# Two graph layers over 128 graphs, float32 in hi and lo halves: an earlier KT_lo, paired h2 copies, a fifth PSUM bank in the ring, and the bias added elsewhere on GpSimd

## The chip, the cores and the metric

One core of a Trainium2 chip. The metric is device time in microseconds, median of the runs shown. Engines: TensorE (PE; its weight loads are PEld), VectorE (DVE), ScalarE (ACT), GpSimd (POOL), SyncE (SP, which issues nearly all DMAs here).

## What is computed

Input x is 128 graphs of 128 nodes with 512 features; adj is a 128x128 0/1 matrix. Two residual layers, each ahead of it a layer norm and a relu:

```python
h = relu(layernorm(x))
z_l, z_g, v = h @ W_lang.T, h @ W_grav.T, h @ W_V.T
A_l = max(zn @ zn.T, 0) * not_eye            # zn: rows of z_l by their norms
A_g = exp(-|z_g[n] - z_g[m]|^2 / (2 sigma^2)) * not_eye
K   = w_l * rows(A_l * adj) + (1 - w_l) * rows(A_g * adj)   # rows: divided by their sum
x   = x + (K @ v) @ W_O.T
h2  = relu(layernorm(x))
x   = x + (adj * adj).T @ h2 + bias
```

## The kernel before, in words

The graphs are taken in groups of four (GB = 4), so there are 32 groups and 32 iterations of one software pipeline; each engine has its own program (the functions `iteration` of SP, POOL, ACT, DVE and PE), and semaphores tie them. Every float32 product is made of three matmuls of fp32r halves (`passes`): hi*hi, hi*lo, lo*hi. A hi half is an ACT copy out of PSUM, a lo half a subtraction on DVE (or GpSimd for h2).

Iteration i on PE, in order:

- **y phase**: eight products y (`y_block`, L947; 3, 3, 6, 6, 9, 9, 12, 12 matmuls of 512 columns) of group i's transposed h with the two triangular halves of the similarity weights. ACT copies each to y_hi (L441), DVE subtracts to y_lo (L590). It waits for all four hT_lo of its group.
- **P phase**: 48 matmuls of 256 columns into p_ps (L994), with the four transposes of K of group i-1 in the middle (L957), which ACT copies to KT_hi (L531) and DVE turns into KT_lo (`kt_lo`, L657).
- **K_v**: K times v for group i-1 (`k_v`, 12 matmuls; waits for KT_lo), which DVE adds to x (`add`, L661).
- **v phase**: four products of 12 matmuls each, h times the folded V and O weights; v_hi on ACT (L478), v_lo on DVE (L590).
- **layer 1** of group i-2 (`layer1`, 12 matmuls), which DVE adds to x (`output`, L694) once GpSimd has added the bias (`add_bias`, L326).

The y, K_v, v and layer 1 products share a ring of four PSUM banks. The uses of the ring are numbered through, 20 in an iteration (8, 4, 4, 4), and `free(use)` (L931) lets PE write a bank once the use BANKS before it has been drained by DVE:

```python
def free(use):
    wait_for(pe, drained, use - BANKS + 1)
```

DVE's order in an iteration: y_lo 0 to 2, `sum_s` of group i-1 (L787), `mask_l`, y_lo 3, `mask_g`, `row_factors` (L635: a reduction and four operations on 128x8), y_lo 4 and 5, `combine` (K), `turn_blocks` 0 and 1 of group i+1, y_lo 6 and 7, `turn_blocks` 2 and 3, `x_stats` of group i+2 (L601, four), `kt_lo` of group i-1, the four `add` with their `stats`, the squared norms of group i (`diagonal`, `squares`), then for each b v_lo, `turned_lo` (hT_lo of group i+1, L610) and for b of 0 and 1 `turn_p`; last the four `output` of group i-2.

GpSimd's order: (L354) wait for both masks of group i-1, four `add_bias` of group i-2 (L326), four `h2_lo` of group i-2 (L341), the norm factors of two layer norms, `row_norms` (L347, L349), `mask_norms` (L332, behind a DMA). It reads x rows, bias and h2f in SBUF, never PSUM.

ACT's order in the v phase: for each b v_hi, then hT_hi of group i+1 (`turned_hi`, L432; the first waits for the DMAs that turn h), behind b = 1 `shift` (L514), and `h2_full` (L502, the second norm and relu) of group i-1:

```python
for k in {0: [], 1: [0], 2: [1, 2], 3: [3]}[b]:
    h2_full(i - 1, k)
```

`add_bias(g, b)` waits for `h2_full(g, b)`, which reads x before the bias is in. SP issues 16 DMAs that turn h blocks (L246) behind `turn_blocks`, the DMAs for P and the norms, the load of x two groups ahead and the stores.

## Time and profile before

| | us |
|---|---|
| median of 3 runs (1272.72 to 1273.73) | 1273.24 |
| the profiled execution, its own time | 1273.49 |
| its span, first to last instruction | 1271.8 |
| PE busy | 1216.1 (96%) |
| DVE busy | 1114.0 (88%) |
| ACT busy | 699.1 (55%) |
| POOL busy | 598.0 (47%) |

The mean granted clock of TensorE is 0.992 of full speed. A matmul's busy time overlaps that of the next, so 96% is the share of the span in which some matmul was in flight; how fast the stream goes is read from the distance between starts. Iterations 2 to 29 look alike. The rows further down are of the one that starts at 603.09 us and ends where the next begins, at 640.76 us.

### The profile page before, as it was taken

Reading aid. Unit: us, or ns where it says so; the run is one execution under the profiler, and the core shown is the slowest. Engines: PE = TensorE matmul, PEld = TensorE weight load, DVE = VectorE, ACT = ScalarE, POOL = GpSimd, SP = SyncE. Lnnn points to the kernel's source line nnn. Section 1 sums busy time; section 2 is a strip of 40 time slices with the busy share of each in tenths; the row PEclk is TensorE's granted clock in tenths of the full one; section 3 lists DMA queues with packets and bytes.
Section 4 is the critical chain, followed back from the end, with each engine's and each line's share of the span. In section 5 each row is a group of like instructions: output and inputs, shape, how many; then the busy total and the mean of one; then the engine's idle time right before and its main releaser. Section 6 shows DMA issues by size and latency. Waiting matters only on the chain.

```text
span 1271.8 us, 22830 instructions
## 1 busy us (share of the span) xinstructions
PE 1216.1 (96%) x6076; PEld 1021.3 (80%) x6076; DVE 1114.0 (88%) x1892; ACT 699.1 (55%) x1324; POOL 598.0 (47%) x991
## 2 busy tenths in 40 slices
PE   7998999999999999999999999999999999999995
PEld 7877888888888888788888888888888888878883
DVE  6577899889889989889989889988988998988878
ACT  6355555565555466555556555546645545655544
POOL 1213455454555554545545445545454554444445
PEclk9998999999999999999999999999999999999997
DMA  7122333434433343433343443343443334343202
GB/s 273 35 90 60 119 101 103 130 121 128 140 102 93 119 126 122 140 108 99 108 134 121 133 128 103 98 125 122 126 140 107 93 113 130 120 138 107 76 33 100
DMA packets 115457, 145.10 MB, mean 114 GB/s; under 512 B 20848, under 2 KB 52720, under 8 KB 115440
## 3 DMA queue, kind: packets, MB, share of 16 engines
q1 hardware_dynamic: 114864, 144.57, 36.7%
q10 hardware_dynamic: 576, 0.33, 0.1%
q8 instruction: 7, 0.11, 0.0%
q14 instruction: 10, 0.08, 0.0%
HBM read 62.46 MB, written 49.87 MB: 88 GB/s over the span
## 4 chain that ended last, share of the span: by engine, by line
PE 42%; DVE 33%; issue 12%; ACT 6%; DMA 2%; DVEq 1%; SPq 1%; POOL 1%; ACTq 0%; POOLq 0%
PE ring L944 40%; DVE h L606 6%; DVE bn L601 5%; DVE deg L637 3%; DVE deg L641 3%; ACT y_hi L441 2%; DVE deg L646 2%; DVE K L651 2%; ACT K L525 2%; DVE chain L787 2%; DVE chain L632 2%; SPq L246 1%; DVE KT_lo L657 1%; DVE x_ring L694 1%; DMA p_dram<-chain 1%
## 5 line engine op out<-in xcount | busy, mean ns | idle before, releaser
L944 PE MATMUL ring<-hT_hi,Lw_hi 128*128 128x512 f32 x640 | 253.8, 397 | 11.9 <-DVE hT_lo L610 5.6
L944 PE MATMUL ring<-hT_lo,Lw_hi 128*128 128x512 f32 x640 | 250.5, 391 | 0.0
L944 PE MATMUL ring<-hT_hi,Lw_lo 128*128 128x512 f32 x640 | 250.4, 391 | 0.0
L326 POOL TENSOR_TENSOR x_ring<-x_ring,bias_sb 128x512 f32 (+1 forms) x124 | 157.5, 1301 | 132.1 <-DVE chain L632 128.3
L441 ACT ACTIVATE y_hi<-ring 128x512 fp32r<-128x512 f32 x256 | 151.4, 592 | 99.3 <-PE ring L944 95.5
L944 PE MATMUL ring<-MT_hi,hT_hi 128*128 128x512 f32 x512 | 199.4, 389 | 1.4 <-DVE MT_lo L590 1.4
L341 POOL TENSOR_TENSOR h_lo<-h2f,h_hi 128x512 fp32r<-128x512 f32 x124 | 156.2, 1292 | 93.0 <-ACT h_hi L509 92.7
L944 PE MATMUL ring<-MT_hi,hT_lo 128*128 128x512 f32 x512 | 199.2, 389 | 0.0
L944 PE MATMUL ring<-MT_lo,hT_hi 128*128 128x512 f32 x512 | 199.2, 389 | 0.0
L590 DVE TENSOR_TENSOR y_lo<-ring,y_hi 128x512 fp32r<-128x512 f32 x256 | 168.9, 680 | 29.7 <-ACT y_hi L441 29.7
L478 ACT ACTIVATE v_hi<-ring 128x512 fp32r<-128x512 f32 x128 | 74.9, 585 | 186.7 <-PE ring L944 186.7
L944 PEld LDWEIGHTS ring<-hT_hi,Lw_hi 128*128 128x128 f32 x640 | 120.7, 189 | 50.7 <-DVE x_ring L694 17.3
L332 POOL TENSOR_TENSOR chain<-rn_cols,mask 128x512 f32<-128x512 f32 x31 | 48.5, 1564 | 224.8 <-DMA rn_cols<-rn_dram 224.8
L994 PE MATMUL p_ps<-y_hi,hT_hi 128*128 128x256 f32 x512 | 147.1, 287 | 0.0
L994 PE MATMUL p_ps<-y_hi,hT_lo 128*128 128x256 f32 x512 | 144.9, 283 | 0.0
L994 PE MATMUL p_ps<-y_lo,hT_hi 128*128 128x256 f32 x512 | 144.8, 283 | 0.0
L944 PEld LDWEIGHTS ring<-hT_hi,Lw_lo 128*128 128x128 f32 x640 | 120.7, 189 | 25.6
L944 PEld LDWEIGHTS ring<-hT_lo,Lw_hi 128*128 128x128 f32 x640 | 120.9, 189 | 23.8
L661 DVE TENSOR_TENSOR x_ring<-ring,x_ring 128x512 f32 (+1 forms) x128 | 86.1, 687 | 51.2 <-PE ring L944 41.9
L590 DVE TENSOR_TENSOR v_lo<-ring,v_hi 128x512 fp32r<-128x512 f32 x128 | 86.2, 674 | 34.2 <-ACT v_hi L478 34.0
L944 PEld LDWEIGHTS ring<-MT_hi,hT_hi 128*128 128x128 f32 x512 | 96.1, 188 | 21.7 <-DVE MT_lo L590 1.8
L432 ACT ACTIVATE hT_hi<-h_turned 128x512 fp32r<-128x512 f32 x124 | 77.4, 625 | 63.8 <-DMA h_turned<-h 55.5
(165 smaller groups left out, 2604.4 us busy)
## 6 DMA issues: line engine op xcount, KB each, us to landing
x_ring<-in_x SPq DMA_DIRECT2D x32, 1024.0 KB, 5.2
out<-x_ring SPq DMA_DIRECT2D x128, 256.0 KB, 2.5
h_turned<-h SPq DMA_DIRECT2D x496, 64.0 KB, 2.0
p_dram<-chain SPq DMA_DIRECT2D x62, 256.0 KB, 2.3
h<-p_dram SPq DMA_DIRECT2D x248, 64.0 KB, 2.5
rn_cols<-rn_dram SPq DMA_DIRECT2D x31, 256.0 KB, 3.7
x_ring<-in_L_gnn_W_lang SPq DMA_DIRECT2D x4, 256.0 KB, 5.5
h2f<-in_L_gnn_W_grav SPq DMA_DIRECT2D x1, 1024.0 KB, 8.9
```

Of the source, the lines that this page charges most:

```text
L326: pool.tensor_tensor(x_rows(g, b), x_rows(g, b), bias_sb[:, :], ALU.add).then_inc(x2b_ready, 1)
L332: pool.tensor_tensor(rn_mask, rn_cols[:, :, :].rearrange("p m b -> p b m"), by_row, ALU.mult)\
L341: pool.tensor_tensor(h2[1][:, b], h2f[:, b], h2[0][:, b].bitcast(F32), ALU.subtract)\
L432: act.activation(hT_columns(0, b), h_columns(b), ACT.Copy).then_inc(ht_hi, 1)
L441: act.activation(y[0][:, a, :, l], bank(n).rearrange("p (b m) -> p b m", b=GB), ACT.Copy)\
L478: act.activation(v[0][:, b], bank(n), ACT.Copy).then_inc(hi_ready, 1)
L590: return dve.tensor_tensor(out, ps, part(hi), ALU.subtract)
L601: dve.bn_stats(bn1[:, b], x_rows(g, b)).then_inc(bn1_done, 1)
L606: dve.transpose(blocks, blocks).then_inc(blocks_ready, 1)
L661: dve.tensor_tensor(x_rows(g, b), bank(n), x_rows(g, b), ALU.add).then_inc(drained, 1)
L944: mm = pe.matmul(out, lhsT, rhs, start=(k == 0), stop=(k == len(terms) - 1))
L994: mm = pe.matmul(p_ps[:, b].rearrange("p l m -> p (l m)"), lhsT, rhs, start=(a == 0 and k == 0 and b % 2 == 0), stop=(a == C - 1 and k == ...
```

## The change

Five edits. `kt_lo(i - 1)` goes ahead of `x_stats(i + 2)` in DVE's order. The ring has a fifth bank, taken from r_ps, which now shares kt_ps's bank (r_ps is used in the last iteration alone); the numbers of the uses move so that 20 uses still begin at bank 0, and a few waits of the setup and of the end follow. ACT's `h2_full` come in pairs behind hT_hi 2 and 3. GpSimd adds the bias for group i-1 behind `row_norms(i)`, where it added it for group i-2 behind the masks. In the last `iteration` GpSimd adds none; the group 30's bias stays with DVE (L699).

```diff
-BANKS = 4
+BANKS = 5
...
-    SETUP = C
+    SETUP = C + 1
...
-        return SETUP + GB + PER * i
+        return SETUP + GB + 1 + PER * i
...
         p_ps = ctx.enter_context(nc.psum_tensor("p_ps", [P, GB, 2, P], F32))
-        r_ps = ctx.enter_context(nc.psum_tensor("r_ps", [P, GB, P], F32))
         kt_ps = ctx.enter_context(nc.psum_tensor("kt_ps", [P, GB, P], F32))
+        r_ps = kt_ps
...
-        side = [p_ps[:, 0:2].rearrange("p b l m -> p (b l m)"), p_ps[:, 2:4].rearrange("p b l m -> p (b l m)"),
-                r_ps[:, :, :].rearrange("p b m -> p (b m)"), kt_ps[:, :, :].rearrange("p b m -> p (b m)")]
+        side = [ring[:, BANKS - 1], p_ps[:, 0:2].rearrange("p b l m -> p (b l m)"),
+                p_ps[:, 2:4].rearrange("p b l m -> p (b l m)"), kt_ps[:, :, :].rearrange("p b m -> p (b m)")]
...
             def iteration(i, before=True, lag=True, after=True, x_next=True):
                 if lag:
-
-                    pool.wait_ge(a_ready, 2 * i)
-                    for b in range(GB):
-                        add_bias(i - 2, b)
                     for b in range(GB):
                         h2_lo(i - 2, b)
                 if after and x_next:
...
                 row_norms(i)
                 if before and not after:
                     norm2(i - 1)
+                if before and after:
+                    for b in range(GB):
+                        add_bias(i - 1, b)
                 if after:
                     mask_norms(i)
...
                     if before and after:
-                        for k in {0: [], 1: [0], 2: [1, 2], 3: [3]}[b]:
+                        for k in {0: [], 1: [], 2: [0, 1], 3: [2, 3]}[b]:
                             h2_full(i - 1, k)
...
                     turn_blocks(i + 1, 2)
                     turn_blocks(i + 1, 3)
+                    if before:
+                        kt_lo(i - 1)
                     if x_next:
                         x_stats(i + 2, 0, GB)
...
                 if before:
-                    kt_lo(i - 1)
                     add(i - 1, 0, n)
...
-                output(g, b - 1, b - 1)
-            output(g, GB - 1, GB - 1)
+                output(g, b - 1, 2 * GB + b - 1)
+            output(g, GB - 1, 3 * GB - 1)
...
+                        if not before and n == BANKS - 1:
+                            pe.wait_ge(side_split, C + 1)
                 wait_for(pe, p_copied, 2 * i)
+                if not before:
+                    pe.wait_ge(side_split, 2 * C)
...
-                layer1(g - 1, b, b, use + GB + b)
+                layer1(g - 1, b, GB + b, use + GB + b)
             for b in range(GB):
-                layer1(g, b, b, use + 2 * GB + b, last=True)
+                layer1(g, b, 2 * GB + b, use + 2 * GB + b, last=True)
```

Left out of the diff above: `first_hi` written with C, `lw_lo`'s and `t_lo`'s last increments of `drained` by 2, which count a use that the setup does not make, and PE's first wait written as `first_use(0)`.

## Rows read from the trace of the kernel before

**Rows 1.** The page: busy time, share of the span, instructions, of the matmuls.

```profile
PE 1216.1 (96%) x6076; PEld 1021.3 (80%) x6076; DVE 1114.0 (88%) x1892; ACT 699.1 (55%) x1324; POOL 598.0 (47%) x991
```

**Rows 2.** Waits of the whole run: total us, times, longest.

```profile
PE ring L944 <- DVE KT_lo L657: 21.6, 28, 0.8
...
PE ring L944 <- DVE x_ring L694: 5.4, 28, 0.3
```

**Rows 3.** Timeline, TensorE, one iteration: start us, us, engine, line, what, [idle <-releaser].

```profile
603.09 0.50 PE L944 MATMUL ring<-hT_hi,Lw_hi 128*128 128x512 f32 x1 [0.23 <-DVE x_ring L694]
...
616.81 0.28 PE L994 MATMUL p_ps<-y_hi,hT_hi 128*128 128x256 f32 x1
...
622.87 0.28 PE L994 MATMUL p_ps<-y_hi,hT_lo 128*128 128x256 f32 x1
...
623.94 0.49 PE L944 MATMUL ring<-v_hi,KT_hi 128*128 128x512 f32 x1 [0.79 <-DVE KT_lo L657]
...
637.45 0.39 PE L944 MATMUL ring<-MT_hi,hT_lo 128*128 128x512 f32 x1
...
640.18 0.40 PE L944 MATMUL ring<-h_hi,A_lo 128*128 128x512 f32 x1
...
640.76 0.50 PE L944 MATMUL ring<-hT_hi,Lw_hi 128*128 128x512 f32 x1 [0.18 <-DVE x_ring L694]
```

**Rows 4.** Timeline, VectorE, the same iteration.

```profile
607.37 1.28 DVE L787 TENSOR_TENSOR chain<-h,chain 128x512 f32<-128x512 f32 x2
...
620.79 2.43 DVE L601 BATCH_NORM_STATS2 bn<-x_ring 128x6 f32 x4
623.14 0.67 DVE L657 TENSOR_TENSOR KT_lo<-kt_ps,KT_hi 128x512 fp32r<-128x512 f32 x1
...
625.10 1.33 DVE L661 TENSOR_TENSOR x_ring<-ring,x_ring 128x512 f32 x2 [1.29 <-PE ring L944]
...
637.26 0.67 DVE L610 TENSOR_TENSOR hT_lo<-h_turned,hT_hi 128x512 fp32r<-128x512 f32 x1
...
639.43 0.68 DVE L610 TENSOR_TENSOR hT_lo<-h_turned,hT_hi 128x512 fp32r<-128x512 f32 x1
```

**Rows 5.** One line each: count, min/median/max ns, first and last start.

```profile
L641 DVE TENSOR_SCALAR deg<-deg x32: 171/1214/1222, 82.2 to 1238.6; 128x8 f32<-128x8 f32 x32
...
L646 DVE TENSOR_TENSOR deg<-deg,wr x32: 168/970/975, 82.7 to 1239.1; 128x8 f32<-128x8 f32 x32
```

**Rows 6.** Timeline, GpSimd, the same iteration.

```profile
605.21 1.55 POOL L332 TENSOR_TENSOR chain<-rn_cols,mask 128x512 f32<-128x512 f32 x1 [6.71 <-DMA rn_cols<-rn_dram]
...
610.96 5.05 POOL L326 TENSOR_TENSOR x_ring<-x_ring,bias_sb 128x512 f32 x4 [4.20 <-DVE chain L632]
...
635.73 0.48 POOL L349 TENSOR_TENSOR wr<-rn,w 128x8 f32<-128x8 f32 x1
```

**Rows 7.** Timeline, ScalarE, the same iteration.

```profile
620.46 0.58 ACT L531 ACTIVATE KT_hi<-kt_ps 128x512 fp32r<-128x512 f32 x1
...
629.71 0.60 ACT L478 ACTIVATE v_hi<-ring 128x512 fp32r<-128x512 f32 x1 [5.93 <-PE ring L944]
...
632.38 0.63 ACT L432 ACTIVATE hT_hi<-h_turned 128x512 fp32r<-128x512 f32 x1 [2.07 <-DMA h_turned<-h]
...
635.08 0.81 ACT L502 ACTIVATE h2f<-x_ring,ln 128x512 f32 x1
635.79 0.58 ACT L478 ACTIVATE v_hi<-ring 128x512 fp32r<-128x512 f32 x1
636.27 0.62 ACT L432 ACTIVATE hT_hi<-h_turned 128x512 fp32r<-128x512 f32 x1
636.79 1.52 ACT L502 ACTIVATE h2f<-x_ring,ln 128x512 f32 x2
```

**Rows 8.** Timeline, VectorE, end of the run.

```profile
1262.68 1.77 DVE L688 TENSOR_TENSOR h_lo<-h2f,h_hi 128x512 fp32r<-128x512 f32 x1
...
1265.11 1.02 DVE L688 TENSOR_TENSOR h_lo<-h2f,h_hi 128x512 fp32r<-128x512 f32 x1
```

More of the change, by code:

```diff
@@ L39, in gnn_pair @@
     G_USES = 2 * C
-    SETUP = C
+    SETUP = C + 1
     PER = G_USES + GB + GB + GB
     def first_use(i):
-        return SETUP + GB + PER * i
+        return SETUP + GB + 1 + PER * i
     HI_PER = G_USES + GB
     def first_hi(i):
-        return SETUP + GB + HI_PER * i + (C if not isinstance(i, int) or i else 0)
+        return C + GB + HI_PER * i + (C if not isinstance(i, int) or i else 0)
     x_g = x.rearrange("(g b) n d -> g n b d", b=GB)
@@ L871, in factor_lo, with lw_lo @@
                                       ALU.subtract).then_inc(side_split, 1)
-            def lw_lo(l, banks, hi_done, done):
+            def lw_lo(l, banks, hi_done, done, last=1):
                 for c in range(C):
@@ L880, in lw_lo @@
                             op0=ALU.mult, op1=ALU.subtract)
-                    e.then_inc(done, 1)
+                    e.then_inc(done, last if c == C - 1 else 1)
             for c in range(C):
@@ L887, in _ @@
             x_stats(0, 0, GB)
-            lw_lo(0, [bank(c) for c in range(C)], hi_ready, drained)
+            lw_lo(0, [bank(c) for c in range(C)], hi_ready, drained, last=2)
             dve.wait_ge(ident_ready, 4)
@@ L906, in _ @@
             for b in range(GB):
-                t_lo(b, SETUP + b, SETUP + b + 1).then_inc(drained, 1)
+                t_lo(b, SETUP + b, C + b + 1).then_inc(drained, 1 if b < GB - 1 else 2)
             dve.wait_ge(a2_hi, 1)
@@ L1006, in iteration @@
                     pe.wait_ge(w_split, 3 * C)
-                    pe.wait_ge(side_split, 2 * C)
                     for c in range(C):
@@ L1059, in _ @@
                 mm.then_inc(setup_mm, 1)
-            pe.wait_ge(drained, SETUP + GB)
+            pe.wait_ge(drained, first_use(0))
             iteration(0, before=False, lag=False)
```

## The prediction

> **What bounds the kernel now.** I read the page first, then the waits, then the timelines of one iteration, engine by engine. The page has PE busy for 96% of the span [rows 1]; PE cannot be relieved here, since the change takes no matmul away, so what is to be had is PE's pauses. The waits name two that come back 28 times each: PE waits for KT_lo ahead of K_v, and for a free bank (behind `output`, L694) ahead of the next y phase [rows 2]. What they cost is read from the starts of matmuls, not from the idle column, since ends overlap [rows 3]. The 60 matmuls of the y phase take 616.81 - 603.09 = 13.72 us, of which 0.11 is the slow first one (0.50 against 0.39 us), so one each 0.227 us. The last P matmul starts at 622.87, and 0.12 later, at 622.99, K_v could start; it starts at 623.94. That is 0.95 us, and 0.11 for the slow first one again: 1.06. The last matmul of layer 1 starts at 640.18; the next y phase could start at 640.41 and starts at 640.76: 0.35 + 0.11 = 0.46. The iteration takes 37.67 us, and without both pauses 36.15.
>
> Why KT_lo is late: on DVE it stands behind the four `x_stats` (620.79 to 623.2, KT_lo at 623.14) [rows 4], though KT_hi is there at 621.04 [rows 7]. And the work ahead of it is slow: two operations on 128x8 take 1.21 and 0.97 us in the middle of the run, and 0.17 at their fastest [rows 5]. They lie under GpSimd's four bias additions (610.96 to 616.01) [rows 6].
>
> **The change, part by part.** The sum is made against the profiled execution (1273.49, span 1271.8); the median, 1273.24, is 0.25 us below it and I take the sum off the median. All engines have slack except PE, so I follow what PE waits for. I count from K, the start of the first K_v matmul when nothing holds it. From the old trace an event behind K_v stands at its time less 623.94 and less 0.11.
>
> *KT_lo ahead of x_stats.* It can start when the turns end (620.79 at the latest) and KT_hi is there, 621.04, and is done by about 621.75, 1.2 us before PE wants it. `x_stats` then end near 624.1; `add` 0 is wanted at 625.10 - 1.06 = 624.04, so it is late by 0.1 at most, and PE does not wait for it. `norm1`, next behind `x_stats` on GpSimd, is needed an iteration later. Gain: 28 x 1.06 = 29.7 us.
>
> *Bias out of the y phase.* It gives DVE back 1.04 + 0.80 us in front of K [rows 5], by which K, the turns and the 16 DMAs that turn h start earlier (until the turns meet the last y_lo, which PE sets). This alone would also end the wait for KT_lo, so beside the first edit it is worth nothing more; it is cover.
>
> *Five banks.* The next y phase then needs v_lo 3 drained instead of `output` 0, and the y product behind it `output` 0. v_lo 3 comes ahead of hT_lo 3, at 639.43 already done in the old trace [rows 4]. The bank wait goes: 28 x 0.46 = 12.9 us. What is late next is hT_lo 3, which PE wants before any y phase: unblocked it ends at 640.11, 0.30 ahead of 640.41. That is all the margin there is.
>
> *Bias behind `row_norms`.* This puts four GpSimd instructions of 1.26 us (5.05 for four) [rows 6] beside hT_lo 2 and 3, which read two SBUF operands. The trace has such a meeting at its end: an h_lo of that same shape takes 1.77 us instead of 0.68 when a bias addition got in first, and the next one behind another bias addition ends at 1266.13, 1.68 after it [rows 8]. When do they meet? GpSimd is free at 636.21, K + 12.16 [rows 6]. `h2_full` 0 now follows hT_hi 2. v 0's last matmul starts 36 x 0.227 = 8.16 before 637.45, at 629.29, and its v_hi starts 0.42 later [rows 7]; v_hi 2 can thus start 0.42 behind v 2's last matmul (K + 10.68), at K + 11.10 (hT_hi 0 waits for the DMAs until 632.38 now and about 1.5 us less after, which keeps ACT in time). Then 0.48 to hT_hi 2, 0.52 to `h2_full` 0, 0.81 for it [rows 7] and 0.08 to GpSimd: bias 0 starts at K + 12.99. hT_lo 2 wants to start at 637.26, K + 13.21. So the bias is first by 0.22 us. hT_lo 2 ends at 12.99 + 1.77 = 14.76, v_lo 3 fits in (v_hi 3 is there at K + 14.4), and hT_lo 3 ends at 14.76 + 1.68 = 16.44. The y phase could start at K + 16.36 (640.41) and starts at 16.48: 0.12 + 0.11 = 0.23 us, at 29 starts (iterations 3 to 31) 6.7 us, and one hit of about 0.6 at iteration 2, which waits for hT_lo anyway. Behind the additions GpSimd has `mask_norms`, for which DVE's `mask_l` waits: bias 2 and 3 end 2.4 us into the y phase; `mask_norms` started 2.12 into it (605.21) [rows 6] and now ends 3.9 into it, ahead of `sum_s` at 4.28 [rows 4].
>
> *Paired h2 copies.* v_hi 2 no longer stands behind `h2_full` 0 (635.08) [rows 7], 0.7 us earlier; PE has its bank anyway. Taken at nothing by itself; what it does is set the start of bias 0, above.
>
> *Setup and end.* The setup waits for lo halves made long before. The end is DVE's chain of single steps, untouched. The nearest price is one meeting of the kind of [rows 8], 1.1 us: taken as 0, bounds -1.1 and +1.1 for each of the two.
>
> Sum: 29.7 + 12.9 - 6.7 - 0.6 = 35.3 us; 1273.24 - 35.3 = 1237.9, say **1238**.
>
> One thing more about such a meeting. In [rows 8] one subtraction and one addition take 1.68 us in turn, less than their own 1.26 + 0.67 = 1.93, so an addition seems to hold DVE for some 1.1 us only, not for all of its time. The Trainium skill (SBUF — State Buffer, SBUF: two separate sides) says that the second pair of ports, which VectorE shares with GpSimd, is an exclusive lock that the first comer keeps for its whole instruction. That VectorE stops behind GpSimd the trace agrees with (1.77 against 0.68 us); what a lock for the whole instruction would give is worked out as rival 2.
>
> **The rivals.** A measurement of this kernel can tell about 0.2%, 2.5 us, from no change.
>
> 1. *hT_lo 2 wins.* If bias 0 starts 0.22 us later than I have it (ACT late by one DMA or `shift`), hT_lo 2 goes first, bias 0 runs beside v_lo 3, and hT_lo 3 ends near K + 15.5. No pause at all: 42.6 - 0.6 = 42 us, 1231. Only 0.22 us decide. 25%.
> 2. *The addition blocks for all of its time.* hT_lo 2 ends at 12.99 + 1.93 = 14.92, hT_lo 3 at 16.85: 0.53 + 0.11 = 0.64 us at 29 starts, 18.6; 1273.2 - 42.6 + 18.6 + 0.6 = 1250. For it: ends of GpSimd are only roughly known. Against: the 1.68 us. 12%.
> 3. *Part of the gain does not come:* KT_lo's pause goes, and another takes the bank's place in full (`add` 0 late, or `output` 0 late for the second y product, for which 0.2 us are left): 29.7 less 5, 1248. For: every margin here is 0.1 to 0.3 us. 8%.
> 4. *Slower.* GpSimd's queue of additions keeps DVE out until all four are through, as it would if DVE could not get in between two. Place: hT_lo 2 in the v phase. It then ends at 12.99 + 5.05 + 0.67 = 18.7, hT_lo 3 1.2 later: 3.7 us of pause at 29 starts, +107, against -42.6: 1338. It decides from a pause of 42.6 / 29 = 1.47 us, hT_lo 3 ending beyond K + 17.7. Against: in the y phase four additions in a row held DVE for one of them at a time (1.22, then 0.97) [rows 5, 6]. With any other loss past that point (a lower granted clock): 4%.
> 5. *It does less than it says:* the ring's fifth bank is not reached or KT_lo's pause stays, 1260 to 1273. The conditions are plain in the code. 2%.
>
> The forecast itself has 49%. **The numbers.** 1238 is the likeliest case. Down, the range reaches past rival 1 (1231) by setup and end: 1229. Up it takes in rivals 2 and 3 (1250): 1251. Left out are rivals 4, 5 and tails, some 10%. Faster by over 0.2%: 0.95; within: 0.01; slower: 0.04.
>
> **What would show it.** Right: no wait of PE for KT_lo; KT_lo done over a microsecond before K_v; the 128x8 operations at 0.17 us; iterations of 36.4 us; PE's wait for L694 replaced by a short one for hT_lo (L610), which has some of 1.2 to 1.8 us; bias additions beside them, some of 1.7 us. Rival 1: the same with iterations of 36.15 us and no wait for L610. Rival 2: 36.8 us. Wrong altogether: iterations of 37 us or more, or a new wait inside the y or v phase.

## The result and the profile after

| | median us | range | ratio to the kernel before |
|---|---|---|---|
| before, same session | 1273.27 | 1272.72 to 1273.73 | |
| the change | 1252.98 | 1249.00 to 1253.60 | 0.9834 [0.9813, 0.9855] |

The forecast was 1238, its range 1229 to 1251. The kernel is faster, as forecast, but by 20.3 us and not 35.3, and its median is 2 us above the range. The profiled execution is the fastest of the four: 1249.0, with a span of 1247.3, so 24.5 below the old span.

The page, the line of busy times of the changed kernel (against [rows 1]):

```profile
PE 1204.8 (97%) x6076; PEld 1018.8 (82%) x6076; DVE 1102.0 (88%) x1892; ACT 715.3 (57%) x1324; POOL 624.8 (50%) x991
```

The waits of the whole run (total us, times, longest; against [rows 2]):

```profile
DVE KT_lo L657 <- ACT KT_hi L531: 47.5, 32, 2.6
...
PE ring L945 <- DVE hT_lo L610: 15.4, 30, 3.5
...
PE ring L945 <- DVE h_lo L688: 10.0, 2, 9.9
```

PE's two repeated waits, for KT_lo and for `output` (L694), are gone. One has come: for hT_lo, 30 times. Now TensorE's timeline of one iteration (start, us, what, idle before and releaser; against [rows 3]):

```profile
592.28 0.49 PE L945 MATMUL ring<-hT_hi,Lw_hi 128*128 128x512 f32 x1 [0.34 <-DVE hT_lo L610]
...
612.08 0.28 PE L999 MATMUL p_ps<-y_hi,hT_lo 128*128 128x256 f32 x1
612.20 0.40 PE L945 MATMUL ring<-v_hi,KT_hi 128*128 128x512 f32 x1
...
629.07 0.49 PE L945 MATMUL ring<-hT_hi,Lw_hi 128*128 128x512 f32 x1 [0.36 <-DVE hT_lo L610]
```

K_v follows the last P matmul after 0.12 us at full speed: that pause is gone. Both y phases (first and last row) start late; the last starts at 629.07, where the matmul before it would have let it start at 628.56. So the new pause is 0.51, and 0.10 for the slow first matmul: 0.61. The iteration takes 629.07 - 592.28 = 36.79 (36.77 over many), against 37.70 before and 36.38 forecast.

VectorE and GpSimd beside it. VectorE, the second half of the v phase (against [rows 4]):

```profile
610.25 0.69 DVE L657 TENSOR_TENSOR KT_lo<-kt_ps,KT_hi 128x512 fp32r<-128x512 f32 x1 [1.49 <-ACT KT_hi L531]
...
625.43 1.78 DVE L610 TENSOR_TENSOR hT_lo<-h_turned,hT_hi 128x512 fp32r<-128x512 f32 x1
627.14 0.68 DVE L590 TENSOR_TENSOR v_lo<-ring,v_hi 128x512 fp32r<-128x512 f32 x1
627.74 1.19 DVE L610 TENSOR_TENSOR hT_lo<-h_turned,hT_hi 128x512 fp32r<-128x512 f32 x1
```

GpSimd, the same stretch, the first three of four additions (against [rows 6]):

```profile
625.37 1.29 POOL L327 TENSOR_TENSOR x_ring<-x_ring,bias_sb 128x512 f32 x1 [1.00 <-ACT h2f L502]
626.61 1.78 POOL L327 TENSOR_TENSOR x_ring<-x_ring,bias_sb 128x512 f32 x1
628.32 1.76 POOL L327 TENSOR_TENSOR x_ring<-x_ring,bias_sb 128x512 f32 x1
```

ScalarE, what releases them (against [rows 7]):

```profile
620.28 0.63 ACT L432 ACTIVATE hT_hi<-h_turned 128x512 fp32r<-128x512 f32 x1 [1.81 <-DMA h_turned<-h]
...
624.33 1.51 ACT L502 ACTIVATE h2f<-x_ring,ln 128x512 f32 x2
```

Here one reads the whole new wait. Bias 0 starts at 625.37, hT_lo 2 asks at 625.43, 0.06 us later. It takes 1.78 us where it needs 0.67, so it got its operands at 625.43 + 1.78 - 0.67 = 626.54, 1.17 after bias 0 began. It is the same for hT_lo 3: bias 1 was itself held by hT_lo 2 to about 627.10 (1.78 for 1.29), and hT_lo 3 got in at 628.26, 1.16 behind. It ends at 628.93, and PE starts 0.14 later. An addition of 1.29 us thus keeps a subtraction out for 1.17.

The small operations are as foreseen: those of [rows 5] are at their shortest in the middle of the run too.

```profile
L641 DVE TENSOR_SCALAR deg<-deg 128x8 f32<-128x8 f32 x32 | 5.5, 172 | 1.1
...
L646 DVE TENSOR_TENSOR deg<-deg,wr 128x8 f32<-128x8 f32 x32 | 5.3, 167 | 1.1
```

**Where the 24.5 us come from.** Three cuts of both traces at the same work, the start of the y phase of iteration 2 and of K_v for group 31. Before: 110.28 and 1244.82; after: 112.81 and 1219.30. The middle is 28.05 us shorter, the setup 2.53 longer, and the end 1.0 longer (26.98, then 28.00). The setup, TensorE in iteration 0:

```profile
34.45 0.50 PE L945 MATMUL ring<-hT_hi,Lw_hi 128*128 128x512 f32 x1 [2.42 <-DVE h_lo L871]
```

The fifth bank holds a block of W_O in the setup; its lo half (L871, from 33.72) is made behind the four of W_V (L863, 30.69 to 33.2) and one y_lo, and the fifth y product waits for it. At the end, VectorE's chain of single steps meets GpSimd:

```profile
1229.05 2.63 POOL L327 TENSOR_TENSOR x_ring<-x_ring,bias_sb 128x512 f32<-128x512 f32 x2 [0.93 <-ACT h2f L502]
...
1230.45 1.25 DVE L677 SCALAR_TENSOR_TENSOR ln<-ln 128x2 f32<-128x2 f32 x1
```

That step on 128x2 took 0.16 us before; now the second of two bias additions lies over it. Such a step of 1.25 or 1.26 us, about 11 us behind the start of K_v for group 31, stands in every trace with five banks, also with the bias in its old place (e2, e7), and in none with four, also with the bias moved (e6, e12). So it comes with the fifth bank and not with the bias's move.

### The profile page after: what moved, and what is told of

Same layout as the page of the kernel before. It is cut to its first block, busy times and chain, and to the rows that moved or that the text cites. A ratio compares the mean times of both kernels' runs of the same rounds, so it can differ in the third digit from the quotient of the medians.

```text
span 1247.3 us, 22945 instructions
## 1 busy us (share of the span) xinstructions
PE 1204.8 (97%) x6076; PEld 1018.8 (82%) x6076; DVE 1102.0 (88%) x1892; ACT 715.3 (57%) x1324; POOL 624.8 (50%) x991
## 4 chain that ended last, share of the span: by engine, by line
PE 88%; DVE 7%; issue 1%; ACT 1%; SPq 1%; DVEq 1%; DMA 0%; POOL 0%; ACTq 0%; POOLq 0%
PE ring L945 71%; PE p_ps L999 14%; DVE hT_lo L610 3%; PE kt_ps L958 1%; SPq L247 1%; PE ring L1043 1%; DVE bn L664 0%; DVEq L694 0%; DVE v_lo L590 0%; DMA x_ring<-in_L_gnn_W_lang 0%; ACT h2f L502 0%; DVE x_ring L661 0%; DVE x_ring L699 0%; ACT h L420 0%; PE ring L1052 0%
## 5 line engine op out<-in xcount | busy, mean ns | idle before, releaser
L327 POOL TENSOR_TENSOR x_ring<-x_ring,bias_sb 128x512 f32 (+1 forms) x124 | 183.9, 1513 | 32.7 <-ACT h2f L502 32.6
L610 DVE TENSOR_TENSOR hT_lo<-h_turned,hT_hi 128x512 fp32r<-128x512 f32 x124 | 130.8, 1055 | 0.6 <-ACT hT_hi L432 0.6
L945 PEld LDWEIGHTS ring<-MT_hi,hT_lo 128*128 128x128 f32 x512 | 96.1, 188 | 19.9
L945 PEld LDWEIGHTS ring<-MT_lo,hT_hi 128*128 128x128 f32 x512 | 96.1, 188 | 19.9
```

Source lines behind the costliest of these rows:

```text
L327: pool.tensor_tensor(x_rows(g, b), x_rows(g, b), bias_sb[:, :], ALU.add).then_inc(x2b_ready, 1)
L610: dve.tensor_tensor(hT_columns(1, b), h_columns(b), part(hT_columns(0, b)), ALU.subtract)\
L945: mm = pe.matmul(out, lhsT, rhs, start=(k == 0), stop=(k == len(terms) - 1))
```

## The experiments

All were timed in turn with the kernel before on the same chip (its medians: 1272.8 to 1273.6). "Iteration" is the distance of two y phases in the middle of the run.

| run | what | median us (range) | ratio [95%] | iteration us |
|---|---|---|---|---|
| e1_again | the change once more | 1251.24 (1250.83 to 1253.33) | 0.9836 [0.9819, 0.9852] | 36.77 |
| e2_bias_old | change, bias back behind the masks | 1240.42 (1239.96 to 1242.90) | 0.9751 [0.9735, 0.9767] | 36.47 |
| e3_bias_hold | change, bias waits for hT_lo 2 | 1235.62 (1231.56 to 1235.98) | 0.9697 [0.9681, 0.9714] | 36.16 |
| e4_setup | change, the late lo half first | 1247.48 (1247.27 to 1248.32) | 0.9803 [0.9787, 0.9820] | 36.77 |
| e5_kt_alone | before, KT_lo earlier | 1273.55 (1272.64 to 1274.01) | 0.9998 [0.9988, 1.0008] | 37.70 |
| e6_bias_alone | before, bias moved | 1268.48 (1268.30 to 1269.63) | 0.9963 [0.9951, 0.9976] | 37.50 |
| e7_banks_alone | before, five banks | 1263.64 (1260.69 to 1264.84) | 0.9918 [0.9900, 0.9936] | 37.17 |
| e8_single | change, h2 copies single | 1259.51 (1256.82 to 1259.77) | 0.9884 [0.9867, 0.9900] | 36.98 |
| e10_hold_setup | e3 and e4 together | 1229.93 (1228.87 to 1230.49) | 0.9658 [0.9645, 0.9671] | 36.14 |
| e11_no_kt | change, KT_lo back | 1249.01 (1248.32 to 1253.86) | 0.9817 [0.9801, 0.9833] | 36.77 |
| e12_bias_hold | before, bias moved with the wait, pairs | 1244.23 (1243.05 to 1244.55) | 0.9770 [0.9757, 0.9784] | 36.65 |
| e13_nudge | change, one small GpSimd step ahead | 1253.12 (1249.05 to 1254.23) | 0.9835 [0.9821, 0.9849] | 36.77 |
| e14_nudge2 | two of them | 1257.45 (1257.19 to 1257.82) | 0.9874 [0.9859, 0.9889] | 36.93 |
| e15_nudge4 | four of them | 1230.91 (1229.71 to 1233.16) | 0.9671 [0.9658, 0.9684] | 36.13 |

My first theory was the prediction's own with its sizes mended: PE waits because bias 0 gets in ahead of hT_lo 2. The rival: something else in the moved work, the shared resource apart, makes the v phase late; and for what misses outside the iterations, the setup's lo half.

**e1_again.** The changed kernel, unchanged.

> The changed kernel once more, to have a second trace of it. Its runs spread from 1249.0 to 1253.6 us, those of before by 1.0 us. If the spread comes from the granted clock, this trace shows about 4 us more time in stretches at 0.5 than the first one (which had some 3 us of it at iteration 2 and some 15 us in the tail), and iterations of 36.77 us as in the first. If it comes from the order of bias 0 and hT_lo 2, which start only 0.06 us apart, some iterations are 36.15 us long and others 36.77, and the waits for hT_lo are fewer than 29.

In 27 iterations in a row hT_lo 2 took 1.78 to 1.80 us and hT_lo 3 1.17 to 1.19. So the order is the same each time, and the spread between executions (1249 to 1254) does not come from an order that changes. The granted clock accounts for part of it, though not in the place where the expectation looked for it. The wait for the fifth bank in the setup is in this trace too, but behind it TensorE runs at half speed:

```profile
35.44 0.50 PE L945 MATMUL ring<-hT_hi,Lw_hi 128*128 128x512 f32 x1 [2.41 <-DVE h_lo L871]
...
38.22 0.63 PE L945 MATMUL ring<-hT_lo,Lw_hi 128*128 128x512 f32 x1
```

From 35.9 to 39.3 us the granted clock is 0.50 (1.2 GHz); in the first trace of the change it is 1.00 there. The way from the first y phase to the second takes 49.65 us here and 48.00 there.

Each run below leaves one trace. Of the ten traces of kernels with this wait, six have such a stretch behind it (e1, e3, e7, e8, e13, e14: 49.45 to 49.65 us on that way) and four have not (the change, e2, e11, e15: 48.00 to 48.02). Of the six traces without the wait (before, e4, e5, e6, e10, e12: 45.28 to 45.40) none has it. The trace of e13, whose iterations are those of the change, is 4.1 us longer than the change's first one. Of these, 1.6 lie here, and 1.4 in iteration 2, where its clock is 0.50 for 6.8 us instead of 3.4. Of the executions of the change without a trace only the mean granted clock is known: 0.990 for the three at 1252.7 to 1253.6, 0.992 for the one at 1249.0. Why the clock falls in some executions and not in others is not shown.

**e2_bias_old.** The additions go back to where they were before:

```diff
                 if lag:
+                    pool.wait_ge(a_ready, 2 * i)
+                    for b in range(GB):
+                        add_bias(i - 2, b)
...
-                if before and after:
-                    for b in range(GB):
-                        add_bias(i - 1, b)
```

> The changed kernel with GpSimd's bias additions back behind the masks; KT_lo early, five banks and paired copies stay. Theory (the additions hold hT_lo 2 and 3 in the v phase, and PE pauses 0.61 us for them at 29 starts): hT_lo takes 0.68 us everywhere, iterations 36.15 us, 17.7 us less than the change, about 1235; the operations on 128x8 take 1.2 and 1.0 us again and cost nothing, since KT_lo has over a microsecond in hand. Rival one (hT_lo 3 is late by its place in DVE's order, whoever holds the port): the pause stays, 1253. Rival two (the y phase cannot bear the additions, KT_lo is late again): a wait for KT_lo of some tenths, 1240 to 1260.

It is 10.8 us faster than e1: the moved bias costs time beside the other edits. Its hT_lo take 0.66 to 0.72 us, and KT_lo is never waited for. Against the theory (36.15 us an iteration, 1235) it misses by 5 us: a smaller pause is left. The start of the y phase and the transfers ahead of it, in three views, TensorE, ScalarE, and SyncE's queue:

```profile
623.58 0.39 PE L945 MATMUL ring<-h_hi,A_lo 128*128 128x512 f32 x1
623.99 0.49 PE L945 MATMUL ring<-hT_hi,Lw_hi 128*128 128x512 f32 x1
```

```profile
616.83 0.63 ACT L432 ACTIVATE hT_hi<-h_turned 128x512 fp32r<-128x512 f32 x1 [3.10 <-DMA h_turned<-h]
```

```profile
605.35 10.03 SPq L247 DMA_DIRECT2D h_turned<-h  x16
```

With the bias under the 128x8 operations again (1.21 and 0.97 us), the turns end later, the 16 DMAs are issued from 605.35 and the first hT_hi starts 11.48 behind, at K + 9.37 instead of K + 8.08 (K is 607.46 here). From there ScalarE works without a break, v_hi 3 comes at 621.95, and the hT_lo 3 behind it ends at 623.85, 0.04 after PE could have started: a pause of 0.18 + 0.11.

**e3_bias_hold.** The additions stay where the change has them, but wait for hT_lo 2:

```diff
                 if before and after:
+                    pool.wait_ge(ht_lo, GB * i + 3)
                     for b in range(GB):
                         add_bias(i - 1, b)
```

> The changed kernel with one wait more: GpSimd starts bias 0 only when hT_lo 2 is done, so that hT_lo 2 goes first by construction. In the changed kernel bias 0 started 0.06 us ahead of it. Theory: hT_lo 2 takes 0.68 us, bias 0 runs beside v_lo 3, hT_lo 3 is held by 0.1 us or so and ends 0.7 us ahead of what PE needs: iterations 36.15 us, 1235. The later end of the additions holds sum_s by up to 1 us in the next y phase, which has that slack. Rival (the additions have no good place in the v phase at all, bias 0 holds hT_lo 3 for nearly its whole time): the pause shrinks only by half, 1244.

15.6 us faster than e1, by one wait more (by the iterations 28 times 0.61 = 17.1 us). VectorE, then GpSimd, one iteration:

```profile
621.38 0.67 DVE L611 TENSOR_TENSOR hT_lo<-h_turned,hT_hi 128x512 fp32r<-128x512 f32 x1
622.62 0.69 DVE L591 TENSOR_TENSOR v_lo<-ring,v_hi 128x512 fp32r<-128x512 f32 x1 [0.56 <-ACT v_hi L479]
623.22 1.00 DVE L611 TENSOR_TENSOR hT_lo<-h_turned,hT_hi 128x512 fp32r<-128x512 f32 x1
```

```profile
622.37 1.30 POOL L327 TENSOR_TENSOR x_ring<-x_ring,bias_sb 128x512 f32 x1 [2.04 <-DVE hT_lo L611]
623.63 1.74 POOL L327 TENSOR_TENSOR x_ring<-x_ring,bias_sb 128x512 f32 x1
```

Bias 0 lies beside v_lo 3, which reads PSUM and takes its usual 0.69. hT_lo 3 asks at 623.22 while bias 0 runs, gets in at 623.55 (1.18 behind bias 0's start again), and bias 1 stands behind it. PE has no pause at all in the middle of the run: 36.16 us, the floor that the prediction put at 36.15.

**e4_setup.** In iteration 0, `factor_lo(C)`, the lo half of the block in the fifth bank, ahead of the four of W_V:

```diff
                         if not before and n == 1:
+                            factor_lo(C)
                             for q in range(C):
                                 factor_lo(q)
                         if not before and 2 <= n <= 3:
-                            factor_lo(C + 2 * n - 4)
+                            if n == 3:
+                                factor_lo(C + 2)
                             factor_lo(C + 2 * n - 3)
```

> The changed kernel with one step of DVE's setup moved: in iteration 0 the lo half of the W_O block that lies in the fifth bank is made ahead of the four lo halves of W_V, not behind them. Theory (the fifth bank was in use by the setup, and PE waited 2.42 us for it at its fifth y product): that pause goes, iteration 1 and all behind it start 2.5 us earlier, 1250.5 against 1253.0. Rival (PE only meets another wait of the setup, for W_V's halves or for hT_lo of group 1): 1253.

The wait of 2.42 us is gone, and the median is 3.8 below e1's. From the first y phase to the second it takes 45.28 us: 2.7 less than in the first trace of the change, and 4.4 less than in e1's, whose stretch at half clock is gone too.

**e5_kt_alone.** On the kernel before, only the first edit:

```diff
                     turn_blocks(i + 1, 3)
+                    if before:
+                        kt_lo(i - 1)
                     if x_next:
                         x_stats(i + 2, 0, GB)
...
                 if before:
-                    kt_lo(i - 1)
                     add(i - 1, 0, n)
```

> The kernel before with KT_lo ahead of x_stats and nothing else. As the prediction priced it: the wait for KT_lo goes, 28 times 1.06 us, 1243. Rival, formed from the trace of before after the result: a loop through the DMAs set the iteration as well. In the iteration of the rows turn_blocks end at 620.86, the 16 DMAs are issued and landed 11.5 us later (632.38), ACT then works without a break to v_hi 3 (638.20), DVE takes v_lo 3, hT_lo 3 and output 0 (640.72) and PE starts at 640.76; 17.77 + 11.52 + 8.38 = 37.67 us, the whole iteration, with no slack. KT_lo's place touches none of it: the pause at K_v goes, the pause behind layer 1 grows from 0.46 to 1.5 us, and the time stays at 1273.

Nothing: 0.9998 [0.9988, 1.0008]. The wait for KT_lo is gone, K_v starts 0.12 behind P, and the iteration is 37.70 as before. Its waits of PE, and the place in TensorE's timeline:

```profile
PE ring L945 <- DVE v_lo L590: 21.7, 29, 1.0
PE ring L945 <- DVE x_ring L694: 6.9, 29, 0.3
```

```profile
638.97 0.50 PE L945 MATMUL ring<-h_hi,A_hi 128*128 128x512 f32 x1 [0.74 <-DVE v_lo L590]
...
640.17 0.50 PE L945 MATMUL ring<-hT_hi,Lw_hi 128*128 128x512 f32 x1 [0.22 <-DVE x_ring L694]
```

The time has moved to the last product of layer 1, which waits for the bank of v_lo 3. So there was a second limit, as long as the first, and it can be added up from the old trace: from the start of the y phase to the issue of the 16 DMAs 620.89 - 603.09 = 17.80, from there to hT_hi 0 (632.38) 11.49, and from hT_hi 0 over ScalarE's unbroken row, v_lo 3, hT_lo 3 and `output` 0 to the next y phase (640.76) 8.38. Together 37.67: the whole iteration. PE can start K_v as early as it likes; the transfers, which start with the turns, do not come earlier.

**e6_bias_alone.** On the kernel before, only the bias moved behind `row_norms`, without the wait.

> The kernel before with GpSimd's bias additions behind row_norms and nothing else (four banks, KT_lo behind x_stats, h2 copies single). DVE gets 2 us back ahead of K and the turns, and the turns end 1.5 us earlier in the iteration. By the loop through the DMAs: this alone ends the wait for KT_lo (19.3 us into the iteration against 19.9) and shortens the loop by 1.5 us; what is left is the bank wait of some 0.3 us, iterations of 36.4 to 36.5 us, 1236 to 1240. By the prediction's account (KT_lo's wait goes, the bank wait stays at 0.46 and the additions hold hT_lo 2 and 3, so output 0 comes another 0.6 us later): iterations of 37.2 us, 1260.

Missed by 30 us. The waits of PE, and VectorE and GpSimd in the v phase:

```profile
PE ring L943 <- DVE x_ring L693: 30.5, 29, 1.1
```

```profile
635.37 1.75 DVE L609 TENSOR_TENSOR hT_lo<-h_turned,hT_hi 128x512 fp32r<-128x512 f32 x1
```

```profile
632.33 5.93 POOL L326 TENSOR_TENSOR x_ring<-x_ring,bias_sb 128x512 f32 x4
```

The wait for KT_lo is gone here too, without its edit: the turns end earlier. But with single h2 copies the row of additions starts 1.1 us ahead of hT_lo 2, and its third addition gets in just ahead of hT_lo 3: 1.75 us, and with four banks `output` 0 must follow before PE may start.

**e7_banks_alone.** The change with only its fifth bank: bias, KT_lo and h2 copies as before.

> The changed kernel with the fifth bank only: KT_lo behind x_stats, the bias behind the masks and the h2 copies single, as before. By the loop through the DMAs: it ends at hT_lo 3 in place of output 0, one DVE instruction (0.61 us) less, iterations of 37.06 us and a pause of PE for hT_lo; with 2.5 us lost in the setup and 1 us in the tail, 1273 - 17.5 + 3.5 = 1259. By the prediction's account (the bank wait of 0.46 us simply goes, KT_lo's stays, 37.21 us): 1273 - 12.9 + 3.5 = 1263.5; the two are told apart by the iteration and by whether PE waits for hT_lo (L610).

Here the prediction's account holds and the loop's misses: the bank's wait goes, KT_lo's stays (20.1 us, 28 times), no repeated wait for hT_lo comes, and the iteration is 37.17, near the account's 37.21 and not the loop's 37.06. With setup and end, 1273.55 (before, same session) - 12.9 + 3.5 is 1264.2, against 1263.6 measured. But the loop is just behind. In this trace it takes 17.73 us from the start of the y phase to the first issue, 11.49 to hT_hi 0, 5.82 to v_hi 3, 1.90 to the end of hT_lo 3 and 0.14 for PE to start: 37.08, only 0.1 less.

**e8_single.** The change with the old `{0: [], 1: [0], 2: [1, 2], 3: [3]}`.

> The changed kernel with ACT's h2 copies as before (one behind hT_hi 1, two behind 2, one behind 3), all else as changed. The prediction took the pairs as free and wrote that they set the start of bias 0. Theory: single copies are ready before GpSimd is done with row_norms, so bias 0 starts at about K + 12.2, in front of hT_lo 2 (K + 13.2) by a whole microsecond; hT_lo 2 waits only 0.1 to 0.2 us for its end, hT_lo 3 again little, and is done near K + 15.9, ahead of the K + 16.36 at which PE wants it: no pause, iterations of 36.15 us, 1251 - 17.7 = 1234. Then the pairs cost what the other edits gain. Rival (v_hi 2 and 3 behind the copies are late and PE waits for v_lo 3 or hT_lo 3 all the same): 1245 to 1255.

Missed as well, theory and rival: 8.3 us slower than e1. hT_lo 2 escapes (0.75 us), and hT_lo 3 takes 1.75, as in e6. The pairs, which the prediction took at nothing, are worth 0.21 us an iteration by where they put the additions, 5.9 us in 28. Another 2.3 us lie between the y phases of iterations 1 and 2 (38.88 us against 36.55 in e1), where this trace has one more stretch at a granted clock of 0.50, from 79.1 to 82.6 us; e14's has the same.

**e11_no_kt.** The change with `kt_lo` back behind `x_stats`.

> The changed kernel with KT_lo back behind x_stats, all else as changed. By the loop and the trace of the change: the turns end at 608.75 there, x_stats would end at 611.1 and KT_lo at 611.8, 0.4 us ahead of the 612.20 at which K_v starts, so KT_lo's place is worth nothing beside the bias's: 1251, no wait for KT_lo. By the prediction's account its move is worth 29.7 us unless the bias's move covers it too, which the prediction said; the prediction would be wrong in a new way if a wait for KT_lo came back (1255 to 1280), for instance because KT_lo behind x_stats delays the adds.

No wait for KT_lo, 36.77 us: beside the moved bias the early KT_lo is worth nothing.

**e12_bias_hold.** The kernel before with the bias moved as in e3 (with its wait) and the paired copies, but four banks and the late KT_lo.

> The kernel before with three of the edits in their smallest form: the bias behind row_norms, held until hT_lo 2 is done, and the paired h2 copies. Four banks, KT_lo behind x_stats. Theory: KT_lo comes in time, hT_lo 3 ends near K + 15.9 as in the held version with five banks, output 0 near K + 16.5, and PE pauses some 0.15 + 0.11 us for it: iterations of 36.4 us, and none of the fifth bank's losses in the setup and the tail: 1273.5 - 29 x 1.27 = 1236.5. Then the fifth bank is worth 0.25 us an iteration, no more. Rival (with four banks the bank wait returns in full, 0.6 us or more, or KT_lo is late): 1245 to 1255.

Iterations of 36.65 for 36.4, and 1244.2 for 1236.5: missed, and 0.8 us below the rival's 1245. There is no wait for KT_lo; the bank's wait comes back in full, TensorE:

```profile
625.67 0.50 PE L944 MATMUL ring<-hT_hi,Lw_hi 128*128 128x512 f32 x1 [0.21 <-DVE x_ring L694]
```

So beside a well placed bias the fifth bank is worth 0.49 us an iteration, about its 0.46 in the old trace. (e3 differs from e12 by KT_lo's place too, but PE waits for KT_lo in neither.)

**e10_hold_setup.** e3 and e4 together, five rounds.

> Both repairs at once on the changed kernel: bias 0 waits for hT_lo 2 (alone 15.6 us less than the change) and the W_O block in the fifth bank gets its lo half first (alone 3.8 us less). They touch different stretches, so they should add: 1251.2 - 15.6 - 3.8 = 1231.8, iterations of 36.15 us in which PE never pauses, and no pause at the fifth y product. Rival (they share a cost, for instance the stretch at half clock behind iteration 1): 1234 to 1236.

1229.93, 1.9 us below the sum of the two repairs, 3.4% below the kernel before and 1.8% below the change: the lowest median here. e15 below comes within 1.0 us of it without the repair of the setup; the two together were not run.

**e13_nudge, e14_nudge2, e15_nudge4.** e3 takes both subtractions out of the way and does not tell which order does the harm. So useless multiplications of 128x4 put bias 0 off (one, two, four of them; here two, without the line that makes the tile `spare`):

```diff
                 if before and after:
+                    pool.wait_ge(h2_done, GB * (i - 1) + 1)
+                    pool.tensor_tensor(spare[:, 0], neg_half[:, :], quarter[:, :], ALU.mult)
+                    pool.tensor_tensor(spare[:, 1], neg_half[:, :], quarter[:, :], ALU.mult)
                     for b in range(GB):
                         add_bias(i - 1, b)
```

> The changed kernel with one useless GpSimd multiplication of 128x4 (about 0.2 us, its result is not used) between h2 copy 0 and bias 0: no wait on DVE is added, bias 0 is only a little later. In the changed kernel bias 0 starts 0.06 us ahead of hT_lo 2. Theory (which of the two comes first at the shared port decides): bias 0 now starts some 0.15 us behind hT_lo 2, hT_lo 2 takes 0.68 us, hT_lo 3 less than 1.1, iterations of 36.15 us, 1235 to 1236, as with the explicit wait. Rival (0.06 us is a coincidence; the additions cost in the v phase whatever the order, and the explicit wait helped by moving them by 0.85 us): 1245 to 1251.

One multiplication did not separate anything: it ran in the 0.23 us that GpSimd leaves between ScalarE's end and bias 0, and bias 0 was still 0.05 us first. So its time, 1253.1, does not decide between theory and rival.

> As the run with one useless GpSimd multiplication of 128x4 ahead of bias 0, but with two. One moved bias 0 by 0.02 us only, 0.05 us ahead of hT_lo 2. The second should move it by 0.17, to 0.12 us behind hT_lo 2. Theory (the order decides): hT_lo 2 takes 0.68 us, the first addition waits for it, hT_lo 3 is held by 0.3 us and ends before PE wants it, iterations of 36.15 us, 15 us less than with one: 1236 to 1238. Rival (the distance counts): hT_lo 3 ends only 0.1 us or so earlier than with one multiplication, iterations of 36.7 us, 1250.

> The same with four multiplications, bias 0 some 0.5 us later than in the changed kernel. Theory (the order decides): bias 0 waits for hT_lo 2 as before and gets the port at the same moment as with two, so the time is that of two, 1236 to 1238. Rival (the distance counts): between that of two and that of the explicit wait, by steps; if two gave 1250, this gives 1243.

With two, hT_lo 2 is first, and the kernel is slower (36.93). VectorE and GpSimd in one iteration of e14:

```profile
630.96 0.67 DVE L614 TENSOR_TENSOR hT_lo<-h_turned,hT_hi 128x512 fp32r<-128x512 f32 x1
632.19 0.69 DVE L594 TENSOR_TENSOR v_lo<-ring,v_hi 128x512 fp32r<-128x512 f32 x1 [0.56 <-ACT v_hi L482]
632.79 1.80 DVE L614 TENSOR_TENSOR hT_lo<-h_turned,hT_hi 128x512 fp32r<-128x512 f32 x1
```

```profile
631.03 1.76 POOL L328 TENSOR_TENSOR x_ring<-x_ring,bias_sb 128x512 f32 x1
632.75 1.30 POOL L328 TENSOR_TENSOR x_ring<-x_ring,bias_sb 128x512 f32 x1
```

hT_lo 2 gets through 0.07 us ahead of bias 0. But bias 0 then ends just as hT_lo 3 is about to ask, and bias 1 starts at 632.75, 0.04 us ahead of it: hT_lo 3 pays the whole 1.13 and ends at 634.59, where it would have ended at 633.46. With four multiplications bias 0 starts at 617.61, 0.17 behind the end of hT_lo 2; hT_lo 3 asks at 618.61 while it runs, takes 0.84 us (in at 618.78, 1.17 behind bias 0's start) and is ahead of bias 1. The iteration is 36.13, and the time, 1230.9, lies below both expectations. My first theory, that the order of bias 0 and hT_lo 2 decides, falls with e14. What these three runs, e3, e6, e8 and the change have in common: a subtraction pays what is left of the 1.17 us of the addition that holds, anything from 0 to 1.13, and for each of the two subtractions hundredths of a microsecond decide how much that is.

## Why the prediction was wrong

**What held.** The direction; what bounds the kernel (PE's pauses, floor 36.15 us an iteration: 36.13 to 36.16 in e3, e10 and e15); both old pauses gone; KT_lo ready early (610.94, 1.26 us ahead of K_v); the 128x8 operations at 0.17; bias 0 just ahead of hT_lo 2, both hT_lo held, the pause at the start of the y phase. Rivals 4 and 5 did not come. Of rival 3 the size came, a pause as large as the bank's (0.61 us for 0.46), but not by its causes, a late `add` 0 or `output` 0.

**The step that failed: "The y phase could start at K + 16.36 (640.41) and starts at 16.48: 0.12 + 0.11 = 0.23 us".** With K = 612.20 the measured chain is:

| event | forecast | measured |
|---|---|---|
| bias 0 starts | K + 12.99 | 13.17 |
| hT_lo 2 asks | 13.21 | 13.23 |
| hT_lo 2 ends | 14.76 | 15.01 |
| hT_lo 3 ends | 16.44 | 16.73 |
| y phase starts | 16.48 | 16.87 |

The mechanism was right, its size was not: 0.51 + 0.10 = 0.61 us for 0.23. Four small terms went the same way. "0.08 to GpSimd" was 0.23 (h2_full 0 ends 0.81 behind 624.33, at 625.14, and bias 0 starts at 625.37; small register instructions of 46 to 100 ns stand between, which I take to make the addresses; the multiplication of e13, on fixed tiles, starts 0.08 behind the same release), with ScalarE 0.03 later besides: 0.18. The hold from the start of an addition was taken from the one meeting of [rows 8], and is 0.07 longer. The second one adds 0.04, and PE starts 0.14 behind hT_lo 3, where I had left 0.04: 0.10. Together 0.39; over 28 iterations 10.9 us of the 15 that are missing. An odd thing follows from e14 and e15: being later was not itself the harm. Later by 0.13 us (from 0.06 ahead of hT_lo 2 to 0.07 behind), bias 0 makes the pause larger still; later by 0.90 (e15), it makes it go.

**The setup and the end, taken as 0.** "The setup waits for lo halves made long before" was wrong: the block in the new fifth bank is split only behind the four of W_V. I had looked at what the new waits name, not at where in VectorE's order the named work stands. The wait is 2.4 us in the trace and the setup 2.5 longer, more than the bound of 1.1. In six of ten traces a stretch at half clock behind it costs 1.5 to 1.6 us more (e1). The end, "untouched", cost 1.0 us within its bound: VectorE's steps are as before, but with five banks one more of them lies under a bias addition.

The sum against the spans: 35.3 forecast, 24.5 measured, 10.8 short. Of these, by the iterations (28 times 37.70 - 36.77 = 26.0, where the forecast's terms give 35.3) 9.3, which is the 10.9 less 0.8, since the old iteration is 37.70 over many and not the 37.67 of the one I read, and less 0.83 that the forecast had for its first and last meeting; setup 2.5; end 1.0; the rest of the middle came out 2.0 better (28.05 - 26.0), some of it because the y phase of iteration 2 runs at a granted clock of 0.50 (1.2 GHz) from its start and is back at 0.98 or more from 116 us on in both traces, though it starts 2.5 us later after the change: 5.8 us of it at half clock before, 2.9 after. PE had stood still before it (3.43 and 3.48 us). The median of the change lies 4.0 above its profiled execution. By e1 and e13, stretches at half clock can make 3 us of such a difference; for the executions of the median themselves there is no trace.

**The hidden second limit: right sum, wrong owner.** The prediction credited 29.7 us to the early KT_lo and called the moved bias cover. The opposite is so. Alone, the early KT_lo gives 0 (e5), because the loop over turns and DMAs was just as long; beside the moved bias it gives 0 (e11), because the turns then end earlier and KT_lo with them. It pays only with the bias in its old place, the fifth bank and the pairs: 37.17 (e7) to 36.47 (e2). Between these two runs lie two edits, and what shortens the loop is the pairs: from hT_hi 0 to v_hi 3 ScalarE takes 5.82 us in e7 and 5.12 in e2, since no copy stands ahead of v_hi 2. That is the 0.7 us that the prediction saw and "taken at nothing by itself". With the early KT_lo and single copies the loop would leave 37.08 (an estimate from the rows of e7, not run), so KT_lo alone is worth at most 0.1 us there; the pairs without it would meet the pause at K_v. The sum was right in kind only because the three edits come together. The trace of before had shown it: ScalarE waits for the DMAs ahead of hT_hi 0 in [rows 7] and has hardly a break behind, and that row ends in the very wait for `output` that I priced at 0.46. I had asked of that row only whether it would be in time.

**The rivals.** Rival 1, "hT_lo 2 goes first ... No pause at all", is false as told: in e14 it goes first, and the pause is larger. It left out that bias 1 meets hT_lo 3. Its number (1231) is that of e15, 1230.9, where bias 0 runs beside v_lo 3, as it had said. Rival 2 named 36.8 us an iteration and 1250, both nearly what was measured (36.77, 1253.0), though its reason is only part of it: it lets an addition hold for the whole 1.26, worth 0.41 us more than the forecast, where the longer hold measured gives 0.11 (0.07 + 0.04) and the rest is start and reaction. The Trainium skill (SBUF — State Buffer, SBUF: two separate sides) has the first comer keep the shared ports for its whole instruction; the hold here ends 0.12 us before the addition's recorded end. GpSimd's ends are only roughly known, so this neither confirms nor refutes it to a tenth.

**The range.** It reached to 1251, the end of rival 2, without adding the bounds for setup and end on top of it: 1250 + 1.1 + 1.1 would have been 1252.2, still 0.8 short of the median.

## What to carry to other kernels

Where GpSimd and VectorE both read two operands from SBUF, do not leave their order to a margin of tenths: a semaphore that holds the side with time to spare cost PE nothing and was worth 15.6 us here, while a shift of 0.13 us turned 36.77 us an iteration into 36.93. Before a pause of the critical engine is credited to one edit, go round every loop of the steady state (here over the DMAs) and add up its length: a pause may be covered by a second limit of the same length, and then two edits are worth something only together. When the spread of a kernel grows with a change, compare the granted clock of several of its traces over the whole span, the setup too. When a buffer is taken from elsewhere, follow the first use of it through the setup, down to its place in the order of the engine that empties it.

## What the hardware showed that I had not expected

- An addition on GpSimd (128x512, two SBUF operands, 1.29 to 1.30 us) keeps a subtraction on VectorE that reads two SBUF operands out for 1.17, 1.16, 1.18 and 1.17 us from when it gets in (the change twice, e3, e14). The cost to VectorE is what is left of that, whatever its own size: up to 1.13 us for 128x512, 1.1 for the 128x2 at the end. In the old y phase it fell on L641 too (128x8, 1.21 us for 0.17), a maximum that reads a single SBUF tensor, so two tensor operands are not needed for it. A subtraction in turn delays an addition by 0.44 to 0.49 us (1.74 to 1.78 for 1.29). v_lo, which reads one operand from PSUM, is never held (0.70 us at most in the middle of any run).
- Between two additions in GpSimd's queue VectorE gets in if it already waits; if it asks 0.04 us late, it waits for the whole next one (e14).
- GpSimd starts an addition 0.23 us after ScalarE's release when its addresses are made in the loop; PE starts 0.14 us after the subtraction it waits for, and its first matmul is 0.10 us slower.
- The 16 DMAs cost 11.5 us from the first issue to the first reader in each of these traces (11.49 before, 11.48 in e2, 11.50 in the change): 10.03 to 10.05 of issue, and about 1.5 behind it.
- Behind the 2.4 us for which TensorE stands still in the setup with five banks, the granted clock fell to 0.50 for 3.4 us in six of ten traces, and in none of the six traces without that wait (e1_again).
